# Guards of two query tiles on the halves of TensorE's rows, one maximum for both, and layer 1's near bias on VectorE

## The reference

```python
q = heads(x @ Wq)          # 16 heads of 16 channels, 256 queries a batch
k, v = heads(context @ Wk), heads(context @ Wv)        # 4096 keys a batch
# layer 0: q and k are rms-normed and rotated, scores scaled by D ** -0.5
# layer 1: rel = key - query; scores += rel_bias[bucket(rel)]
attn = softmax(q @ k.T)    # over the 4096 keys
out = (attn @ v) @ Wo
```

## Time and profile before

| | |
|---|---|
| three runs, median (range) | 7272.3 us (7267.72 to 7275.11) |
| the profiled execution | 7272.54 us, span 7270.7 us |
| busy: PE / DVE / ACT / POOL | 83% / 55% / 43% / 15% of the span |
| mean granted clock of PE | 0.902 of full |
| guards, layers 0 and 1 | 2048 products, 394 ns mean, busy 790.6 us |
| their maxima on DVE | 2048 of 128x512, 689 ns mean, busy 1360.2 us |
| layer 0's attention batches | 213 to 538, 538 to 862, 862 to 1186, 1186 to 1437 us |
| layer 1's | 2648 to 2955, 2955 to 3265, 3265 to 3573, 3573 to 3843 us |
| layer 2's | 4521 to 5592 us, four |

### The profile page before, as it was taken

The page is one execution under the profiler, slowest core; times in us unless marked ns, Lnnn a source line. Parts: engine busy times, 40 slices in busy tenths (PEclk is TensorE's granted clock), DMA queues, the critical chain, the costliest instruction groups (busy, mean ns, idle before and its releaser), DMA issues. The chain is left out here.

```text
span 7270.7 us, 100659 instructions
## 1 busy us (share of the span) xinstructions
PE 6009.5 (83%) x35364; PEld 3348.9 (46%) x35364; DVE 3997.9 (55%) x8335; ACT 3123.7 (43%) x7764; POOL 1100.0 (15%) x1170
## 2 busy tenths in 40 slices
PE   5799898877388279999998897888877998987887
PEld 2344443333255145455445554333333565556754
DVE  5566576648211336666672333988987445525631
ACT  3455565510133035455452112988987224532211
POOL 4333231013433421001000002110100000001100
PEclk8899999978699699999998898999988678998998
DMA  3333231120488342223110113322311000021100
GB/s 113 95 84 94 79 98 58 56 92 1 147 259 257 98 128 79 78 73 86 58 49 30 33 39 110 97 87 82 97 58 58 1 1 7 1 85 66 50 19 25
DMA packets 283464, 550.00 MB, mean 76 GB/s; under 512 B 31966, under 2 KB 189028, under 8 KB 264148
## 3 DMA queue, kind: packets, MB, share of 16 engines
q1 hardware_dynamic: 264628, 493.47, 23.0%
q0 software_dynamic: 18336, 50.09, 1.9%
HBM read 414.73 MB, written 128.75 MB: 75 GB/s over the span
## 5 line engine op out<-in xcount | busy, mean ns | idle before, releaser
L2641 DVE TENSOR_REDUCE t<-banks 128x1 f32<-128x512 f32 x2048 | 1360.2, 689 | 445.2 <-PE banks L2515 381.1
L2731 ACT ACTIVATE t<-banks 128x1024 f32<-128x1024 f32 x1024 | 1048.8, 1024 | 754.5 <-PE banks L2544 749.1
L2962 ACT ACTIVATE t<-banks,t 128x256 f32<-128x256 f32 x2048 | 938.2, 529 | 78.5 <-DVE t L2899 56.5
L2515 PE MATMUL banks<-t 96*128 96x512 bf16 x2048 | 790.6, 394 | 116.4 <-PEq L66 68.1
L2899 DVE TENSOR_REDUCE t<-banks 128x4 f32<-128x1024 f32 x512 | 623.6, 1219 | 97.1 <-PE banks L2845 57.8
L2544 PE MATMUL banks<-t 97*128 97x256 bf16 x4096 | 650.7, 273 | 0.0
L2561 PE MATMUL banks<-t 128*17 128x256 f32 x8192 | 641.9, 385 | 4.9 <-ACT t L2701 2.9
L2962 ACT ACTIVATION_READ_ACCUMULATOR t<-banks,t 128x1 f32 x2048 | 507.6, 261 | 0.0
L2544 PEld LDWEIGHTS banks<-t 97*128 97x128 bf16 x4096 | 390.3, 98 | 231.8 <-issue 92.4
L2515 PEld LDWEIGHTS banks<-t 96*128 96x128 bf16 x2048 | 198.8, 97 | 581.3 <-DVE t L2641 360.0
L2858 PE MATMUL banks<-t 128*17 128x256 f32 x4096 | 326.4, 404 | 158.5 <-DVE t L2910 105.9
(11 more groups left out here) (432 smaller groups left out, 9691.3 us busy)
## 6 DMA issues: line engine op xcount, KB each, us to landing
t<-in_L_ffn_w SPq DMA_DIRECT2D x127, 640.0 KB, 5.7
t<-scratch_k SPq DMA_DIRECT2D x192, 384.0 KB
t<-scratch_k SPq DMA_DIRECT2D x192, 256.0 KB
scratch_k<-t SPq DMA_DIRECT2D x128, 384.0 KB, 15.6
xn_feat<-in_ctxT SPq DMA_DIRECT2D x72, 512.0 KB, 15.9
t<-in_ctxT SPq DMA_DIRECT2D x56, 512.0 KB
scratch_k<-t SPq DMA_DIRECT2D x192, 128.0 KB, 2.4
t<-scratch_k SPq DMA_DIRECT2D x192, 128.0 KB
```

Source lines behind the costliest of these rows:

```text
L2515: mm = nc.tensor.matmul(ps[:, 4 + g % 2, :], qstack[0:SHIFT, h, t * P:(t + 1) * P], kstack[0:SHIFT, slot(h), kc * KC:(kc + 1) * KC], start ...
L2641: nc.vector.tensor_reduce(gm[:, h % 2, g // NK, g % NK:g % NK + 1], ps[:, 4 + g % 2, :], AX.X, ALU.max).then_inc(max_done, 1)
L2731: nc.scalar.activation(p[:, i % 3, :].rearrange("p (b t) -> p b t", b=2), ps[:, 2 * (i % 2):2 * (i % 2) + 2, :], ACT.Exp).then_inc(exp_don ...
L2962: nc.scalar.activation(p[:, i % SL, j * T:(j + 1) * T], ps[:, 2 * (i % 3) + j // 2, (j % 2) * T:(j % 2 + 1) * T], ACT.Exp, bias=nm[:, i % ...
```

## The change

- The rows are stacked anew. Rows 0 to 63 of `kstack` hold key parts 0, 0, 1, 2, row 64 to 95 part 0 twice, row 96 the ones, rows 97 to 112 part 1. `qstack` has the matching query parts 0, 1, 0, 0 and 2 (rows 64 to 79) and 1 (rows 97 to 112), zeros at 80 to 95. A second stack `qguard` has parts 0, 1 and 0 at rows 64, 80 and 97. The full product has 113 rows.
- A guard of tile 0 uses rows 0 to 63, one of tile 1 rows 64 to 112, issued one after the other into banks 4 and 5; DVE takes both maxima in one operation. A pair waits for the maximum of the pair before.
- Layer 1's near bias in the scores is added by three DVE operations (`add_near`), and the exponential of a head's first unit waits for them.
- Keys come in five transfers a head, queries in three plus two for `qguard`. Three more ranges are cleared by GpSimd in the layer norm. Some scratch tiles move into the normalised tile `core.xn`.

```diff
-K_SLOTS = (0, 0, 0, 1, 1, 2)
-Q_SLOTS = (0, 1, 2, 0, 1, 0)
-K_RUNS = ((0, 3), (3, 2), (5, 1))
-SHIFT = SLOTS * D
-ROWS = SHIFT + 1
+K_ROWS = ((0, 0, 2), (1, 2 * D, 1), (2, 3 * D, 1), (0, 4 * D, 2), (1, 6 * D + 1, 1))
+Q_SLOTS = (0, 1, 0, 0, 2, 1)
+Q_ROWS = ((0, 4, 0), (4, 5, 4 * D), (5, 6, 6 * D + 1))
+GUARD_ROWS = ((0, 2, 4 * D), (2, 3, 6 * D + 1))
+SLOTS = len(Q_SLOTS)
+HALF = 64
+SHIFT = 6 * D
+ROWS = 7 * D + 1
...
-    for part, (first, count) in enumerate(K_RUNS):
+    for part, first, count in K_ROWS:
         src = keys[part, h * D:(h + 1) * D, :].unsqueeze(0).to_broadcast([count, D, S])
-        sp.dma_start(kstack[first * D:(first + count) * D, slot, :], src).then_inc(landed, 16)
+        sp.dma_start(kstack[first:first + count * D, slot, :], src).then_inc(landed, 16)
...
+def load_queries(sp, queries, rows, stack, landed):
+    for first, end, row in rows:
+        sp.dma_start(stack[row:row + (end - first) * D], queries[first * D:end * D]).then_inc(landed, 16)
...
     if coming is None:
-        GUARDS, SHIFT_AT = (2, 3, 2, 3, 2, 2, 2, 0), 7
+        PAIRS, SHIFT_AT = (1, 1, 2, 1, 1, 1, 1, 0), 7
     elif rope:
-        GUARDS, SHIFT_AT = (1, 3, 3, 3, 2, 2, 2, 0), 7
+        PAIRS, SHIFT_AT = (1, 1, 2, 1, 1, 1, 1, 0), 7
     else:
-        GUARDS, SHIFT_AT = (3, 3, 2, 2, 3, 3, 0, 0), 6
+        PAIRS, SHIFT_AT = (1, 1, 2, 1, 2, 1, 0, 0), 6
...
+                def guard(h, kc):
+                    if kc == 0:
...
-                    if g >= 2:
-                        pe.wait_ge(max_done, GU * h + g - 1)
+                    if kc >= 1:
+                        pe.wait_ge(max_done, NK * h + kc)
                     biased = bias is not None and kc == 0
-                    mm = nc.tensor.matmul(ps[:, 4 + g % 2, :], qstack[0:SHIFT, h, t * P:(t + 1) * P],
-                                          kstack[0:SHIFT, slot(h), kc * KC:(kc + 1) * KC], start=True, stop=True,
-                                          skip_group_check=biased)
+                    for t, (stack, low, high) in enumerate(((qstack, 0, HALF), (qguard, HALF, ROWS))):
+                        mm = nc.tensor.matmul(ps[:, 4 + t, :], stack[low:high, h, t * P:(t + 1) * P],
+                                              kstack[low:high, slot(h), kc * KC:(kc + 1) * KC], start=True, stop=True,
+                                              tile_position=(low, 0), skip_group_check=biased)
+                        if not biased:
+                            mm.then_inc(scored, 1)
+                    for t in range(QT if biased else 0):
                         for k in range(t + 2):
-                            mm = nc.tensor.matmul(ps[:, 4 + g % 2, k * P:(k + 1) * P], core.identb[:, :],
+                            mm = nc.tensor.matmul(ps[:, 4 + t, k * P:(k + 1) * P], core.identb[:, :],
...
-                        near = [t for t in range(QT) if kt - t <= 1] if bias is not None else []
                         mm = nc.tensor.matmul(out, kstack[:, slot(h), kt * P:(kt + 1) * P], qstack[:, h, :],
-                                              start=True, stop=True, skip_group_check=bool(near))
-                        for t in near:
-                            mm = nc.tensor.matmul(out[:, t * P:(t + 1) * P], core.ident[:, :],
-                                                  bias[0][:, kt - t + 1, h, :], start=False, stop=True,
-                                                  skip_group_check=True)
+                                              start=True, stop=True)
...
-                    for g in guards[0:1]:
-                        guard(h + 1, g)
+                    for kc in guards[0:1]:
+                        guard(h + 1, kc)
                     scores(i)
-                    for g in guards[1:2]:
-                        guard(h + 1, g)
                     if i >= 1:
                         weigh(i - 1)
-                    for g in guards[2:]:
-                        guard(h + 1, g)
+                    for kc in guards[1:]:
+                        guard(h + 1, kc)
...
-                def maxima(h, g):
-                    dve.wait_ge(scored, GU * h + g + 1)
-                    nc.vector.tensor_reduce(gm[:, h % 2, g // NK, g % NK:g % NK + 1], ps[:, 4 + g % 2, :], AX.X,
-                                            ALU.max).then_inc(max_done, 1)
+                def maxima(h, kc):
+                    dve.wait_ge(scored, GU * h + QT * kc + QT)
+                    nc.vector.tensor_reduce(gm[:, h % 2, :, kc], ps[:, 4:4 + QT, :], AX.X, ALU.max).then_inc(max_done, 1)
...
+                def add_near(h):
+                    dve.wait_ge(qk, EU * h + 1)
+                    first = 2 * (EU * h % 2)
+                    unit = ps[:, first:first + 2, :].rearrange("p b (j t) -> p (b j) t", t=P)
+                    for tile, pieces in ((1, (0, 3)), (0, (1,)), (2, (2, 5))):
+                        near = unit[:, pieces[0]:pieces[-1] + 1:3, :]
+                        last = nc.vector.tensor_tensor(
+                            near, bias[0][:, tile:tile + 1, h, :].to_broadcast([P, len(pieces), P]), near, ALU.add)
+                    last.then_inc(biased, 1)
...
                     if h + 1 < H:
-                        for g in units_of[e]:
-                            maxima(h + 1, g)
+                        for kc in pairs_of[e][0:1]:
+                            maxima(h + 1, kc)
+                    if bias is not None and e == 0:
+                        add_near(h)
+                    if h + 1 < H:
+                        for kc in pairs_of[e][1:]:
+                            maxima(h + 1, kc)
...
                     act.wait_ge(qk, i + 1)
+                    if bias is not None and e == 0:
+                        act.wait_ge(biased, h + 1)
...
-                       constants=[(kstack[SHIFT:ROWS, :, :], 1.0), (values[0][:, :, :, D:VW], 1.0),
+                       constants=[(kstack[SHIFT:SHIFT + 1, :, :], 1.0), (qguard[HALF:P, :, :], 0.0),
+                                  *((q[HALF:P, :, :], 0.0) for q in qstacks), (values[0][:, :, :, D:VW], 1.0),
```

More of the change, by code:

```diff
@@ L1987, in project_rope @@
         sb = core.allocator(c_)
[L1988 removed]
+        rest = core.xn[:, 0:4, :].rearrange("p (a b) c -> p a (b c)", a=2)
+        parts, ctx = sb([P, 2, 3, KC], BF16), sb([P, 2, CT, KC])
         tab, raw, mix, square = sb([P, 2, 2, KC]), sb([P, 2, 2, KC]), sb([P, 2, 2, KC]), sb([P, 2, KC])
@@ L2034, in _ @@
                             sp.wait_ge(stored[f], 16 * stores_of(VU + f))
-                        sp.dma_start(first[1][0:SHIFT], first[0]).then_inc(first_in, 16)
+                        load_queries(sp, first[0], Q_ROWS, first[1], first_in)
+                        load_queries(sp, first[0], GUARD_ROWS, first[2], first_in)
                 for f in range(CT):
@@ L2418, in load_keys, with attend_context @@
 def load_keys(sp, keys, kstack, h, slot, landed):
-    for part, (first, count) in enumerate(K_RUNS):
+    for part, first, count in K_ROWS:
         src = keys[part, h * D:(h + 1) * D, :].unsqueeze(0).to_broadcast([count, D, S])
-        sp.dma_start(kstack[first * D:(first + count) * D, slot, :], src).then_inc(landed, 16)
-KEY_DMAS = len(K_RUNS)
+        sp.dma_start(kstack[first:first + count * D, slot, :], src).then_inc(landed, 16)
+KEY_DMAS = len(K_ROWS)
+def load_queries(sp, queries, rows, stack, landed):
+    for first, end, row in rows:
+        sp.dma_start(stack[row:row + (end - first) * D], queries[first * D:end * D]).then_inc(landed, 16)
+QUERY_DMAS = len(Q_ROWS) + len(GUARD_ROWS)
 def keys_loads(h):
     return h // 3 + (h % 3 != 0)
-def attend_context(core, keys, v, qstack, kstack, slot, bias, att, coming=None, following=None):
+def attend_context(core, keys, v, qstack, qguard, kstack, slot, bias, att, coming=None, following=None):
     nc, ps = core.nc, core.ps
@@ L2447, in attend_context @@
     if coming is None:
-        GUARDS, SHIFT_AT = (2, 3, 2, 3, 2, 2, 2, 0), 7
+        PAIRS, SHIFT_AT = (1, 1, 2, 1, 1, 1, 1, 0), 7
     elif rope:
-        GUARDS, SHIFT_AT = (1, 3, 3, 3, 2, 2, 2, 0), 7
+        PAIRS, SHIFT_AT = (1, 1, 2, 1, 1, 1, 1, 0), 7
     else:
-        GUARDS, SHIFT_AT = (3, 3, 2, 2, 3, 3, 0, 0), 6
+        PAIRS, SHIFT_AT = (1, 1, 2, 1, 2, 1, 0, 0), 6
     V_AT = 5 if rope else 4
-    units_of = [range(sum(GUARDS[:e]), sum(GUARDS[:e + 1])) for e in range(EU)]
+    pairs_of = [range(sum(PAIRS[:e]), sum(PAIRS[:e + 1])) for e in range(EU)]
     OUT, SPARE = 6, 7
@@ L2578, in _ @@
                 for g in range(0, GU, 2):
-                    guard(0, g)
-                    guard(0, g + 1)
+                    guard(0, g // 2)
                     if new and rope and g in (2, 4):
@@ L2663, in finish @@
                     last.then_inc(out_done, 1)
-                for g in range(GU):
-                    maxima(0, g)
-                    if new and not rope and g == 9:
+                for kc in range(NK):
+                    maxima(0, kc)
+                    if new and not rope and kc == 4:
```

(5 more changed lines are left out.)

46 lines of the change are left out of this document (22 added, 24 removed).

## The result

The changed kernel takes 7645.88 us (median of 4 runs, 7644.51 to 7649.09) where the kernel before takes 7270.01: a ratio of 1.0518, 95% interval 1.05 to 1.0536. The prediction was 7522 with a range of 7390 to 7670, slower with a chance of 0.88. Sign, mechanism and range held; the loss is 373 us in the profiled execution (span 7643.2 against 7270.7) and not 249, so the time lies outside the 7470 to 7570 that the prediction gave its own mechanism. The mean granted clock of PE is 0.886, was 0.902.

The account below looks back on a forecast made before the run. PE's instruction stream was taken to set a head's length. Heads of layers 0 and 1 (25 + 75 + 26 + 93), clears 17 and transfers 13 gave +249 us on the kernel before: 7522, range 7390 to 7670.

Parts of the forecast that it names:

- its own mechanism: Forecast proper: pairs waiting in a closed loop slow the heads; 7522 us, alone 7470 to 7570, chance 0.67.
- part 2: Cross-attentions of layers 0 and 1: each pair waits for the previous pair's maximum, a loop of 1.73 us, range 1.71 to 1.76.
- The worst unit: Unit of a head with two pairs: PE has nothing to do between loops, so it takes 3.46 us.
- Heads at full clock: Longer heads: layer 0 last batch +25 us, with projections +75; layer 1 last batch +26, with projections +93.
- I leave the clock at full: Assumed no clock loss in these batches, PE being busy some 80%, as layer 2's first batch kept 0.97.
- Rival A: Same loop, no drain between pair and whole-array products, 0.11 us off each open entry: 7440 us, chance 0.13.
- Rival B: The two halves of a pair don't run at once; every loop and pair grows by 0.18 us: 7695, chance 0.11.
- Rival C: Faster: a pair's maximum is back before PE needs the banks, so PE's work alone decides: 7162 us, chance 0.09.
- part 3: Layer 1: near bias on DVE removes 1.13 us a head from PE, adds 1.0 on DVE; mostly given back.
- part 4: Layer norms: three added clears lengthen GpSimd's chain by 5.7 us in each of three layers, +17, bounds 0 and 20.
- part 5: Extra key and query transfers, with layer 2's first pairs of each batch: +13 us, bounds 0 and 35.

Follow-up runs that it names:

- Experiment 5: Changed kernel with each pair's maximum taken over only the first 256 of 512 keys in each bank: 7304.87 us, ratio 1.0051.
- experiment 6: Changed kernel with ten unread products behind the second pair of the two-pair unit, last batches of layers 0 and 1 only: 7611.94 us, ratio 1.0478.
- experiment 7: Changed kernel with one pair in each of a head's eight units and the next head's shift at unit 7: 7472.6 us, ratio 1.0281.
- experiment 3: Changed kernel with half-row guards issued one at a time, each with its own maximum and two banks in turn: 7546.44 us, ratio 1.0374.
- experiment 2: Changed kernel with layer 1's near bias back on PE's identity products, pairs, clears and transfers as changed: 7644.15 us, ratio 1.05.
- experiment 1: Kernel before with only layer 1's near bias moved to VectorE as three additions: 7221.57 us, ratio 0.9933.
- experiment 4: Changed kernel with the three added clears made by VectorE before the norm's statistics instead of GpSimd: 7621.83 us, ratio 1.0481.
- experiment 9: Kernel before with only a head's keys brought in five transfers over 112 rows, the second part again to unread rows: 7285.47 us, ratio 1.0028.

## Why the prediction was right, and where it was short

**The loop** (part 2) was right: 1.73 forecast, 1.72 to 1.75 measured. Experiment 5 changes only its length and takes back 341 us, the clock's loss among them. The worst unit was named rightly too (3.46; 3.48 measured, 1330.58 to 1334.06).

**Heads at full clock** came out as forecast. Layer 0's last batch 15.9 (15.92), with projections 19.3 and 20.9 (19.00 and 20.6), layer 1 20.1 (20.20) and 17.1 (17.41, the 0.37 copy). Priced from these heads, or for the last batches from experiment 6, the loss at full clock is (39.6 - 36.84)/2 x 45 = 62, 21.7, 2.18 x 45 = 98 and 28.9, together 211; the forecast had 219.

**The mis-sized term** is the sentence "I leave the clock at full: PE would be busy some 80% of a batch, as in layer 2's first batch". The heads' loss is 300, not 211, and 89 us of it are the clock: 14.4 and 18.7 in the last batches, shown by experiment 6, and some 32 and 24 in those with projections. These two are what is left over when the full-clock heads are taken off; windows over single heads give a clock of 0.92 there, but no run filled them. The share of some 80% was forecast rightly (an estimated 82% at full clock), but it does not settle the clock: layer 2's first batch kept 0.97 with 81%, layer 1's last batch of experiment 7 kept 0.98 with 80%, and here it was 0.89. The forecast's own working already held the place, a unit of 3.46 us in every head, of which PE works some 1.9 in the trace.

**Rival A** (no drain): refuted by experiment 3. I took 0.11 for the first of the two changes and 0.03 for the second half; it is 0.10 and 0. **Rival B**: refuted by the same rows. **Rival C** (faster): its condition, a maximum that is back before PE needs the banks, was not met. Its price is not refuted. Experiment 5 has the short loop and is still at 1.0051, but it isn't C: each head keeps a wait of 0.82 us at the unit with two pairs (129 us of waits in all), and the clears and transfers stay. Its heads save 0.4 us in layer 0's last batch (13.6 for 13.99) and nothing with projections; without the 0.82, by estimate, it would be 1.2 and 0.75, and C had 0.6. A short loop with one pair in each unit was not run.

**Near bias** (part 3): the additions took 0.95 (1.0 forecast), the stall behind them 1.39 and 0.73 (1.1 and 0.45), the difference being mostly the copy. "Mostly given back" held beside the pairs (experiment 2) and not without them (experiment 1).

**Constants** (part 4): 17 forecast, with bounds of 0 and 20; 28.5 in the trace, 24 by experiment 4, both above the upper bound. The length of a clear was right (3.4; 3.5 measured). Wrong was the step that let them run beside VectorE for free until GpSimd's chain ends last. VectorE's tensor_scalar operations are held until GpSimd's clear ends. The trace of before showed it, in a row that I had not read in this light: an operation on 8 columns of 7.04 us, 0.17 in every norm without such a clear. The Trainium skill (SBUF — State Buffer, "SBUF: two separate sides") has the rule, an exclusive lock on a shared pair of ports that VectorE's two-port modes need; these rows agree with it.

**Transfers** (part 5): 13 forecast, bounds 0 and 35; the rest of the time grew by 44, above the bound, and the keys' transfers alone cost 19 (experiment 9). The sign was wrong for layer 0's last batch: with five transfers PE waits less for keys there (4.2 us, was 8.0), not more. Where layer 2 stands longer, it is behind the projections' own stores:

```profile
5201.40 0.69 DVE L2265 CAST t<-banks 128x512 bf16<-128x512 f32 x1 [3.44 <-DMA scratch_k<-t]
5203.63 1.06 PE L2886 MATMUL banks<-t 128*17 128x256 f32 x8 [4.29 <-DVE t L2938]
```

VectorE waits for a store of the next batch's keys, and its maxima, and PE's weighing, wait behind it: two such stands of 3.5 to 4.3 us in this batch, five in layer 2's four batches, 19.7 us together. Before, none of these waits was over 1.2 us; experiment 9 has them too, up to 3.6.

Two errors of size, 89 and 31, and 12 for the clears, less 8 for the heads, are the 124 us between forecast and profile. That 7646 still lies in the range is in part luck: the range went up to 7670 to take in the lower part of rival B, which did not happen, and the clock filled that room.

## What to carry to other kernels

Merging two operations that shared two buffers in turn makes one buffer of the two. Write down the closed loop (fill, read, release) and compare it with the other engine's work for one round, before counting what the merged operation saves. Where new waits recur on TensorE, read the granted clock of the stretch behind them and price it too: here a unit with 1.35 us of waiting a head, among other waits, cost 0.8 us of clock on top, and useless products in its place made the kernel faster. The busy share of the whole batch did not tell. And take a change apart: one half of this one was worth 0.7% by itself, and was hidden by the other.

## What the runs showed of the hardware

- Two products on the two row halves of TensorE run at once: 0.39 us for both, 0.38 for one. A change between half-row and whole-row products costs 0.10 us each way (guard to scores 0.31 or 0.32 for 0.22, scores to guard 0.54 for 0.43); between half rows and the weighing's column quarters none beyond what 96 rows paid (0.32 both).
- Eight heads with half-row guards kept the half clock after a batch's start, throughout or nearly, one of them with PE busy 25.39 of 26 us (experiment 3); with 96 rows the second head of each batch was at full clock. Not explained.
- PE at a clock of 0.50 takes 0.97 us for four score products and 1.06 for the weighing, where it takes 0.61 and 0.63 at full clock. A wait of 1.35 us a head between waits of 0.25 came with a clock of 0.89, one of 1.39 with 0.33 in front and none behind with 0.98 (experiment 7).
- GpSimd's clear holds VectorE's tensor_scalar operations until it ends, but not its statistics or its own clears. A clear of a contiguous row costs some 0.85 us per 1000 elements, bf16 or fp32 (10.33 for 12288, 5.21 for 6144); the 512 scattered ones of the values take 1.00.
- VectorE clears 64 x 4096 bf16 zeros in 1.76 us, as 2048 words of four bytes, but 1 x 8192 bf16 ones take 6.88: the same 0.84 to 0.86 ns for each element of a row.
